# A decoder layer on one core: the FFN's first two bias adds move behind the products, and the load of tile 3 moves ahead of a weight unit's

## The reference

```python
x = _layernorm(x + _L0_attn_ref(x, L0_attn_w_qkv, L0_attn_w_o))
x = _layernorm(x + _L0_xattn_ref(x, ctx_4096, L0_xattn_Wq, L0_xattn_bq, L0_xattn_Wk, L0_xattn_bk))
x = _layernorm(x + _L0_ffn_ref(x, L0_ffn_qweight, L0_ffn_lut4, L0_ffn_lut8, L0_ffn_bias))
# _L0_ffn_ref: weights from bit planes through a table per row (w_l with 4 bits, w_h with 8), then
y = jnp.where(mask[..., None], y_h, y_l) + bias      # mask: the row's norm is over 64
```

## Time and profile before

| | us |
|---|---|
| median of 3 runs | 1262.35 (1261.17 to 1265.23) |
| the profiled execution | 1258.71 |
| its span, first to last instruction | 1256.9 |
| PE busy | 1229.9 (98%) |
| DVE busy | 862.7 (69%) |
| POOL busy | 615.6 (49%) |
| ACT busy | 580.9 (46%) |
| mean granted PE clock | 0.995 |

### The profile page before, as it was taken

One profiled execution on the slowest core, in us unless ns is written; L12 is line 12 of the kernel. 1 busy time (PEld: TensorE's weight loads), 2 busy tenths in 40 slices (PEclk: granted clock), 3 DMA queues, 4 the chain that ended last, 5 costly groups with the idle time before them and its releaser, 6 DMA issues.

```text
span 1256.9 us, 25026 instructions
## 1 busy us (share of the span) xinstructions
PE 1229.9 (98%) x8134; PEld 1038.3 (83%) x8134; DVE 862.7 (69%) x2510; ACT 580.9 (46%) x1659; POOL 615.6 (49%) x520
## 2 busy tenths in 40 slices
PE   8999999999999999999999999999999999899997
PEld 6888889998788888888877787888888888788886
DVE  7999989565778888788766974354363625866564
ACT  5131213546777877877860121342342524632322
POOL 3522112458676766776750000454456454975552
PEclk9999999999999999999999999999999999999999
DMA  8254535364874344445433112427143354633221
GB/s 287 70 199 138 155 120 203 119 190 133 212 197 144 119 127 145 124 122 144 127 114 136 34 54 102 150 67 268 67 161 109 134 202 151 217 135 118 86 82 67
DMA packets 130833, 173.67 MB, mean 138 GB/s; under 512 B 36672, under 2 KB 91968, under 8 KB 130112
## 3 DMA queue, kind: packets, MB, share of 16 engines
q1 hardware_dynamic: 130752, 172.62, 42.7%
HBM read 115.94 MB, written 56.62 MB: 137 GB/s over the span
## 4 chain that ended last, share of the span: by engine, by line
PE 63%; POOL 15%; issue 11%; DVE 6%; DMA 2%; SPq 1%; ACT 1%; POOLq 0%; DVEq 0%; ACTq 0%
PE bank L775 12%; PE bank L777 12%; PE bank L776 12%; POOL prob L2176 10%; PE bank L861 5%; PE bank L1206 4%; PE bank L1207 4%; PE bank L1208 4%; PE bank L966 2%; POOL att_lo L2182 2%; PE bank L826 2%; PE bank L784 1%; DMA vv<-v_scr 1%; PE bank L903 1%; DVE bits L1674 1%
## 5 line engine op out<-in xcount | busy, mean ns | idle before, releaser
L2176 POOL TENSOR_TENSOR prob<-prob,rinv 128x512 f32<-128x512 f32 x192 | 206.7, 1077 | 148.6 <-DVE rinv L1761 148.6
L1328 ACT ACTIVATE prob<-bank,nmax 128x256 f32<-128x256 f32 (+1 forms) x512 | 211.6, 429 | 77.8 <-DVE nmax L1753 72.1
L1753 DVE CUSTOM_DVE_ANT_0 bank<-bank,mask 128x256 f32<-128x256 f32 (+1 forms) x512 | 170.0, 384 | 37.2 <-PE bank L888 23.0
L903 PE MATMUL bank<-ident,prob 128*128 128x128 f32 x768 | 115.5, 273 | 1.5 <-POOL prob L2176 0.8
L903 PEld LDWEIGHTS bank<-ident,prob 128*128 128x128 f32 x768 | 94.2, 140 | 25.4 <-POOL prob L2176 2.5
L1328 ACT ACTIVATION_READ_ACCUMULATOR prob<-bank,nmax 128x1 f32 x512 | 109.7, 214 | 0.0
L966 PE MATMUL bank<-wo_hi,att_hi 128*128 128x512 f32 x256 | 104.3, 407 | 2.6 <-issue 2.6
L1908 DVE SCALAR_TENSOR_TENSOR k_lo<-bank,bA,k_hi 128x512 fp32r<-128x512 f32 x32 | 24.0, 751 | 120.6 <-ACT k_hi L1461 118.9
L888 PE MATMUL bank<-k,q 96*128 96x256 f32 (+1 forms) x512 | 104.2, 305 | 2.1 <-DMA vv<-v_scr 2.1
L775 PE MATMUL bank<-xc_hi,w_hi 128*128 128x512 f32 x240 | 94.8, 395 | 7.0 <-DVE xc_lo L1616 6.9
L966 PE MATMUL bank<-wo_hi,att_lo 128*128 128x512 f32 x256 | 101.3, 396 | 0.0
(11 more groups left out here) (221 smaller groups left out, 3247.3 us busy)
## 6 DMA issues: line engine op xcount, KB each, us to landing
q<-qk_scr SPq DMA_DIRECT2D x192, 128.0 KB, 2.4
x_st<-x_scr SPq DMA_DIRECT2D x32, 512.0 KB, 4.2
qk_scr<-rot SPq DMA_DIRECT2D x60, 256.0 KB, 2.6
xc_in<-x_cols SPq DMA_DIRECT2D x32, 256.0 KB, 5.0
y<-x SPq DMA_DIRECT2D x16, 512.0 KB, 3.6
x_scr<-y SPq DMA_DIRECT2D x16, 512.0 KB, 2.7
cx_in<-ctx_in SPq DMA_DIRECT2D x16, 512.0 KB, 4.8
x_scr<-x_st SPq DMA_DIRECT2D x16, 512.0 KB, 2.9
```

The lines of the kernel that those rows point to most:

```text
L903: mm = nc.tensor.transpose(tb[:, at * P:(at + 1) * P], prob[:, k % 4, c:c + P], ident[:, :])
L1328: mm = nc.scalar.activation(prob[:, k % 4, i * keys:(i + 1) * keys], SBANK[pos][:, i * keys:(i + 1) * keys], ACT.Exp, bias=nmax[:, k % 4, ...
L1753: mm = nc.vector.tensor_tensor_reduce(part, part, mask[:, 2 * P - keys:2 * P], 1.0, BIGGEST, ALU.add, ALU.min, nmax[:, k % 4, i:i + 1])
L2176: nc.gpsimd.tensor_tensor(pr, pr, rinv[:, k % 4, 0:n].unsqueeze(2).to_broadcast([P, n, keys]), ALU.mult)\
```

## The change

In words: SP's list puts load_x2(3) ahead of load_f(F_B22). POOL's add_bias(0) and add_bias(1) leave their place ahead of pair 0's sums: add_bias(0) comes behind the third sum_low of pair 1, add_bias(1) behind the fourth, and each waits until its tile has all its products (y3_part at C12, at C21). The bias of these two tiles is therefore added last instead of first. DVE doesn't wait for a bias in pair 0 and takes no statistics there; it does so in pair 1, between the C11 add and part_low(1, A22), after a wait for the fourth add_bias. BIAS_TURN gives the place of each tile's add in the new order 2, 3, 0, 1, 4, 5, ... ACT makes part_high(1, A22) ahead of normalise3(0), POOL makes rstd3(0) in pair 1.

```diff
+        BIAS_TURN = {n: at for at, n in enumerate((2, 3, 0, 1) + tuple(range(4, TILES)))}
@@ SP, stage4_last
                 store_x2(g, 1)
-                load_f(F_B22)
                 sp.wait_ge(x2_stored[1], 16 * GROUPS)
                 load_x2(3)
+                load_f(F_B22)
                 sp.wait_ge(acc_done, LAST_ACC + 1)
                 load_f(F_T4)
@@ ACT
+                if q == 1:
+                    part_high(q, A22)
                 normalise3(2 * q - 2)
-                part_high(q, A22)
+                if q > 1:
+                    part_high(q, A22)
                 normalise3(2 * q - 1)
@@ DVE
-                dve.wait_ge(x2b_ready, 2 * q + 1)
+                if q:
+                    dve.wait_ge(x2b_ready, BIAS_TURN[2 * q] + 1)
                 add_part(q, U1_OUT, A11, u, 0, 0)
 
                 dve.wait_ge(y3_part, PARTS * q + U1_OUT)
                 add_part(q, C11_OUT, A12, P2_BANK, 0, 0)
-                half_stats(q, C11_OUT, 0, 0)
+                if q == 1:
+                    dve.wait_ge(x2b_ready, BIAS_TURN[1] + 1)
+                    half_stats(0, C11_OUT, 0, 0)
+                    half_stats(0, U3_OUT, 1, 1)
+                    half_stats(0, C12_OUT, 0, 1)
+                    row_stats(0, 0)
+                    half_stats(0, C21_OUT, 1, 0)
+                    row_stats(0, 1)
+                if q:
+                    half_stats(q, C11_OUT, 0, 0)
                 part_low(q, A22)
...
-                dve.wait_ge(x2b_ready, 2 * q + 2)
+                if q:
+                    dve.wait_ge(x2b_ready, BIAS_TURN[2 * q + 1] + 1)
                 add_part(q, P5_OUT, S1, P5_BANK, 1, 1)
...
-                half_stats(q, U3_OUT, 1, 1)
+                if q:
+                    half_stats(q, U3_OUT, 1, 1)
 
                 add_part(q, C12_OUT, S4, P5_BANK, 0, 1)
-                half_stats(q, C12_OUT, 0, 1)
-                row_stats(q, 0)
+                if q:
+                    half_stats(q, C12_OUT, 0, 1)
+                    row_stats(q, 0)
 
                 add_part(q, C21_OUT, A22, u, 1, 0)
-                half_stats(q, C21_OUT, 1, 0)
-                row_stats(q, 1)
+                if q:
+                    half_stats(q, C21_OUT, 1, 0)
+                    row_stats(q, 1)
@@ POOL
             def add_bias(n):
 
+                if n < 2:
+                    pool.wait_ge(y3_part, (C12_OUT, C21_OUT)[n])
                 pool.wait_ge(x2ps_ready, 2 * n + 2)
...
-            add_bias(0)
             f_unit_low(F_T1, (0,))
             sum_low(0, S2)
             f_unit_low(F_T1, (1,))
             sum_low(0, S1)
-            add_bias(1)
             sum_low(0, S3)
             rstd2(GROUPS - 1, GT - 1)
             sum_low(0, S4)
             for q in range(TWOS):
+                if q == 1:
+                    add_bias(1)
+                    rstd3(0)
                 if q:
                     rstd3(2 * q - 1)
                 if q + 1 < TWOS:
                     add_bias(2 * q + 2)
                     add_bias(2 * q + 3)
                     for i in (S2, S1, S3):
                         sum_low(q + 1, i)
-                rstd3(2 * q)
+                if q == 0:
+                    add_bias(0)
+                else:
+                    rstd3(2 * q)
                 if q + 1 < TWOS:
                     sum_low(q + 1, S4)
             rstd3(TILES - 1)
```

## The result

The changed kernel took 1265.96 us (median of 6 runs, 1264.28 to 1267.71) against 1260.61 for the kernel before (6 runs, 1258.75 to 1265.23, which include the three shown ahead). The ratio is 1.0052, 95% interval 1.0038 to 1.0067: 6.6 us slower, 4.8 to 8.4. (The two medians by themselves are 5.35 us apart, which lies in that interval.) The profiled execution's span is 1263.4 against 1256.9.

A forecast was written before the change was run, and what follows sets the result against it. TensorE (PE), busy for 98% of the span, was taken as the bound. Turning of tile 5 5.3 us later plus 1.4 for the clock: 6.7 slower, 1262.35 + 6.7 = 1269.05, say 1269.0; range 1263.3 to 1271.5.

The forecast's parts named there:

- main step: Pair 1: DVE's wait for the fourth add_bias delays part_low(1,A22), moving the turning of tile 5 5.3 us later.
- Rival D: The stalls go and nothing replaces them, because the bias adds come earlier: 1253.5 for the profiled run; chance 0.03.
- C: Rival: the stall at tile 5 is paid by what the removed stalls give; -0.5 to +0.9 us, chance 0.08.
- clock term: Clock drop after PE's stop at the turning of tile 5: 1.4 us (0, or twice that).
- stall at S3: Pair 0: PE's stall of 2.5 us ahead of S3 and its clock drop of 1.4 go.
- S4 and A22: Pair 0: PE waits for DVE ahead of each, 0.5 to 2.5 us; S4 starts at 1096.75, A22 at 1101.35.
- the pattern I took: Three loads in a row, landing 7.2 and 10.9 us after the first issue: F_B22 lands at 1090.8, F_T4 at 1094.4.
- rival B: The loads are quick: F_B22 landed by 1088.4, its low ahead of add_bias(2); +4.3 with the clock drop, +2.9 without; chance 0.12.
- lock: A DVE operation with two SBUF inputs and a POOL operation exclude each other; without it, U3 2.0 earlier, sum 4.7.

The follow-up runs named there:

- e3: Changed kernel, but in pair 1 DVE makes part_low(1,A22) and the U2 add before waiting for the fourth add_bias and taking the statistics; ratio 1.0001 to the kernel before.
- e8: Changed kernel with add_bias(0) and add_bias(1) over one column instead of 1024; ratio 0.9997 to the kernel before.
- e2: Changed kernel with the old order of SP's loads, so only the bias and statistics of tiles 0 and 1 are moved; ratio 1.0025 to the kernel before.
- e4: Changed kernel, but POOL waits ahead of add_bias(2) until DVE's three f_unit_lows are done; ratio 1.0026 to the kernel before.
- e5: e3 together with e4's wait on POOL; ratio 0.9965 to the kernel before.
- e9: e5, and in pair 1 DVE makes the P5 add ahead of pair 2's part_lows and U3 ahead of sums(2); ratio 0.9959 to the kernel before.
- e10: e9 with the old order of SP's loads (F_B22 ahead of tile 3); ratio 0.9938 to the kernel before, 1252.97 us against 1260.22.
- e11: Kernel before with one swap on POOL, add_bias(1) behind sum_low(0,S3) instead of ahead of it; ratio 1.0010 to the kernel before.
- e1: Kernel before with only the SP edit, tile 3's load ahead of F_B22's; ratio 0.9994 to the kernel before.

## Why the prediction was right
**The main step held.** The turning of tile 5 was forecast 5.3 us late, and is 5.2 late. The links between hold too (in the time of the trace before): POOL's three sum_lows of pair 1 were forecast for 1105.1 and start at 1105.1, add_bias(1) was to end at 1114.9 and ends at 1114.8, part_low(1,A22) at 1119.7 and ends at 1119.5. e3 shows that the place of DVE's wait is the cause, e8 that the two adds of the bias in POOL's list give 4.3 of the 6.1 us of the stop. The rest of the delay hangs on how late U3 comes in pair 0, as e2 shows. Rival D (the wait isn't felt) is out, and so is C: it needed F_B22 and F_T4 by about 1088, and they landed at 1090.0 and 1092.6.

**The clock term was low.** 1.4 was forecast by the stop of 2.53 us in before, 1.8 is measured after the stop of 6.12, within the bound of twice 1.4.

**The stall at S3 went as said, and 2.35 and 1.40 us at S4 and A22 came for it.** The forecast had 2 and 1.8, with S4 at 1096.75 and A22 at 1101.35; with the 0.45 us added by which this trace runs ahead, they are at 1096.98 and 1101.38.

**The loads were faster than the pattern I took.** Tile 3 landed at 1087.3 (forecast 1087.5), F_B22 at 1090.0 (forecast 1090.8, lower bound 1090.0), F_T4 at 1092.6 (forecast 1094.4, lower bound 1092.5). It made no difference, and for F_B22 this was luck: its low part was ready at 1092.11, 0.84 us after POOL had begun add_bias(2) at 1091.27, so it had to wait for the end of that add at 1093.7. Had it been ready 0.9 us sooner, it should have gone first, as rival B has it; no run shows that case. For F_T4 the landing mattered less, since add_bias(3) had been waiting since 1093.7 and went ahead of it, to 1098.1. The Trainium skill, page "SBUF — State Buffer", section "SBUF: two separate sides", gives the rule for this, an exclusive lock for the whole instruction; e4 agrees, with 2.29 against 3.72 and 3.88. Without the lock the forecast would have been 4.7, so the lock was priced at 2.0; e4, which avoids it by order, lies at +3.3 by its ratio and +2.9 by its trace, 3.3 and 4.1 faster than the changed kernel. The lock was priced too low because the loads were put too late: in the time of the trace before, U3 starts at 1096.4 in e4, where the forecast without the lock had 1098.65, waiting for F_T4. With the lock in place the error on the loads didn't reach the sum; without it, it would have.

**The time itself.** 1269.0 was forecast, 1265.96 measured. 1.7 of the 3 us are the base: the three runs shown had a median of 1262.35, the six of the comparison 1260.61. The other 1.3 are the 6.65 that were forecast less the 5.35 between the two medians, and 6.65 lies within the interval of 4.8 to 8.4.

**Open.** Why F_T4 landed 8.1 us after its issue here, where F_T3 took 9.4 in before behind as much, wasn't tried. Nor was the clock's cost by itself: it was read from the traces only. How much of the gain of e5, e9 and e10 the early adds and POOL's wait would bring in before, with the bias where it was, wasn't run either.

## What to carry to other kernels
When work is moved to "behind the products", follow it to the engine that must wait for it, and list what stands behind that wait: here one part_low of 0.6 us, which PE needed for something else, made a free-looking wait of DVE worth 7 us. With the late work where its engine had room the loss of 6.6 was gone (e3), and with one wait that keeps a POOL operation out of DVE's way it became a gain of 4.4 (e5; 1.8 by its trace). Run the parts of a change apart and together: here they cost 0.1 and 2.0 alone and 7.0 together, because one used up the time that paid for the other. A small operation on POOL is not small when DVE is in an operation with two SBUF inputs: 0.26 us became 2.37 in e11.

## What the runs showed of the hardware
A stop of PE doesn't set the clock's price by its length alone. The clock was at 0.50 after stops of 2.53 us (before), 5.07 (e11), 5.70 (e2), 6.12 (after) and 6.54 (e4). After shorter ones it went either way at the very same place, S4 of pair 0: it stayed at 1.00 after 2.35 (after) and 2.21 (e8), and fell after 2.24 (e3), where the fall came 1.5 us after PE had gone on. What decides between the two isn't shown. It stayed at 1.00 even after 3.25, with 3.0 us of work between it and another stop of 1.60:

```profile
1098.00:1101.00 3.00, 2.96 (x13) 2.46 (x14) 2.97 (x6) 0.64 (x3) 3.00 (x2) 1.00 0.71 231
```

That is e1, from the start of S4 on (the same columns as in the earlier trace rows). Nor does the price grow evenly with the stop: 1.4 us in before, 2.4 in e11 (all of S4 at 0.50, 5.28 us instead of 2.83), 1.6 in e2, 1.6 in e4, 1.8 in after. A forecast should hold both cases open for stops of 2 to 3.3 us, as the prediction did for S4, and give the price a range; its single 1.4 for a stop of 6 us was 0.4 too low.
